# Soft mixture of experts in a vision tower: dispatch of three quarters before the fourth, phi normalised in the prologue, combine logits in two parts

## The chip, the core and the metric

The kernel runs as one program on one core of one Trainium2 chip. The core has TensorE (PE, matmuls, with a weight load PEld for each), VectorE (DVE), ScalarE (ACT), GpSimd (POOL) and SyncE (SP, which here only issues DMAs); each works through its own instruction list in order and waits on semaphores. The metric is the device time of one execution in microseconds (us), as the median of several runs.

## The reference

32 images of 49 tokens with 192 channels go through a tower of two layers: patch embedding, a two-way selective scan (Mamba), a soft mixture of 64 experts, then an RWKV-like attention with its feed-forward, and a transformer block with a mixture of 4 experts. The change is at the soft mixture:

```python
xn = _l2norm(x, axis=2)                      # x is layernorm(h), h after the scan layer
phin = scale * _l2norm(phi, axis=0)          # phi: 192 x 64 experts
logits = jnp.einsum('bmd,dnp->bmnp', xn, phin)
d = jax.nn.softmax(logits, axis=1)           # dispatch: over the 49 tokens of an image
c = jax.nn.softmax(logits.reshape(b_, m_, n_ * p_), axis=-1)   # combine: over the 64 experts
xs = jnp.einsum('bmd,bmnp->bnpd', xn, d)     # the slots: one row per image and expert
h = gelu(einsum('bnpd,ndh->bnph', xs, w1) + b1)
ys = jnp.einsum('bnph,nhd->bnpd', h, w2) + b2
y = jnp.einsum('bnpd,bmnp->bmd', ys, c)
```

## The kernel before

All data is float32. The 1568 tokens are cut into 16 tiles of 98 tokens (two images each); four tiles, eight images, are a quarter, and most work goes by quarters q = 0 to 3.

The selective scan runs in 8 stages of 24 units. Each unit is a multiply and a scan on DVE (L1463, L1474), an exponential on ACT (L1034), a multiply on POOL (L821) and two matmuls on PE that add to a state sum in PSUM; after a channel group's last unit DVE multiplies the sum with its gate (L1524), and PE projects the gated rows out (`out_pe`). After the last unit DVE also took phi to unit length (`unit_phi`, L1489 to L1495: square, sum, a reciprocal root by integer trick and three Newton steps on 64x1 elements, multiply).

Then comes what is called the slot stage here. DVE takes layer-norm statistics and the unit-length factors for tiles 0 to 11 (`FIRST`) and afterwards for tiles 12 to 15 (`LAST`). ACT makes the unit-length rows `xn` (L1146), PE turns them (L1885) and ACT copies the turned rows to `xnT`. From there, for each quarter: PE makes the 64 x 392 dispatch logits; DVE takes the maximum over each image's tokens and subtracts it (L1567, L1568); ACT takes the exp (L1157); DVE sums, inverts and multiplies (L1574 to L1576, the "share"); PE turns the shares back (L2085); DVE spreads them into blocks that keep the two images of a tile apart (L1583, `dbd`, the "masked block"). The slot matmuls follow: 12 groups `s_xs` (three channel strides for each quarter), each copied out of PSUM by ACT or DVE in turn (L923, L1588).

The expert layers take 16 groups of 4 experts. In step g, PE does the second layer of group g-2, the first layer (two halves of the 768 hidden channels) of group g, and the turning of group g-1's hidden rows. The combine logits of all 16 tiles stood in step 0, behind group 0's first layer (`combine_logits`, 96x98 weights, 64 columns); their softmax is on DVE and ACT (L1594, L1595, L1191).

SP issues the weights of the experts in this order, with one fixed wait for each piece of buffer space: the first layers of groups 0, 1 and the second layer of group 0 as soon as the scan stage is out; first layer 2 and second layer 1 once phi is turned; then for each g from 3 the first layer of group g when group g-3's first layer is done (`s_h1`), and the second layer of group g-1 when group g-3's output is done (`s_y2`). The first of these second-layer loads waits for `s_y2` 0, the output of expert group 0.

PSUM has 8 banks; a table (`plan`, `use`) fixes which bank every product uses and which engine takes it out, and PE waits before it fills a bank until the former product has been taken.

The small parameters are loaded in the prologue. ACT's first work, the exp of `a_neg` (L941), waits for all loads of the key "small", and its 30 diagonal matrices (L928) follow, then the copies of the first token tiles, for which DVE's first statistics wait.

## Time and profile before

| | us |
|---|---|
| median of 3 runs | 1515.61 |
| lowest and highest run | 1510.67, 1516.45 |
| the profiled execution | 1509.02 |
| its span in the profile | 1507.3 |

| engine | busy us | share of the span | instructions |
|---|---|---|---|
| PE | 1323.9 | 88% | 6684 |
| PEld | 767.2 | 51% | 6684 |
| DVE | 915.8 | 61% | 1513 |
| ACT | 670.9 | 45% | 1206 |
| POOL | 554.6 | 37% | 399 |

The DMA queues moved 151.96 MB; 32 transfers of 2304 KB each are the expert weights. All positions below are us from the start of the span, in one profiled execution. The shares are means over stages with different limits: DVE is busy all the time in the scan stage and PE and DMA in the expert layers. A bracket at the end of a timeline row gives how long the engine was idle before it and which instruction or transfer ended that. A float32 matmul stands as two records in the trace, and a row that is marked x12 is a run of 12 records with a common line and operation.

### The profile page before, as it was taken

The numbers are of one execution on the slowest core, as the hardware profiler recorded it, in microseconds if no ns is written. First come the engines' busy times: TensorE is split into PE (matmuls) and PEld (weight loads), VectorE is DVE, ScalarE is ACT, GpSimd is POOL, SyncE is SP. The second block draws the span as 40 slices with busy tenths as digits, with TensorE's granted clock in tenths as the row PEclk, the third lists the DMA queues.
The fourth block names the chain that finished last, engine by engine and source line by source line (L and its number), as shares of the span: only waits on it lengthen the run. The fifth ranks groups of instructions, "written<-read, shape, count | busy, mean of one in ns | idle before, by whom it ended". The sixth has DMA issues, their size and how long they took to land.

```text
span 1507.3 us, 18440 instructions
## 1 busy us (share of the span) xinstructions
PE 1323.9 (88%) x6684; PEld 767.2 (51%) x6684; DVE 915.8 (61%) x1513; ACT 670.9 (45%) x1206; POOL 554.6 (37%) x399
## 2 busy tenths in 40 slices
PE   7979989898989867469988859979999999999998
PEld 6634445454545434244433445547856659445444
DVE  3789999999999999972100148855446624221022
ACT  4786767677777744042110117631552241313311
POOL 1478898988989887300000020012034302000000
PEclk9999999999999999769999969999999999999999
DMA  6405051422414040344999940000010001030101
GB/s 205 172 2 172 12 162 37 135 75 98 127 46 171 12 160 0 138 178 189 395 397 396 372 103 0 1 0 1 1 38 1 2 1 31 7 110 13 37 0 33
DMA packets 38773, 151.96 MB, mean 101 GB/s; under 512 B 10364, under 2 KB 14587, under 8 KB 33948
## 3 DMA queue, kind: packets, MB, share of 16 engines
q1 hardware_dynamic: 34588, 149.21, 27.6%
q10 hardware_dynamic: 4096, 1.58, 0.4%
q8 instruction: 54, 0.88, 0.2%
q14 instruction: 35, 0.29, 0.1%
HBM read 147.56 MB, written 1.63 MB: 99 GB/s over the span
## 4 chain that ended last, share of the span: by engine, by line
PE 54%; DVE 20%; issue 10%; ACT 6%; DMA 5%; POOL 4%; SPq 1%; ACTq 0%; DVEq 0%; POOLq 0%
PE ps L1876 52%; DVE arena L1474 7%; DVE arena L1463 5%; DMA arena<-in_e_b 4%; POOL arena L821 3%; ACT arena L923 2%; ACT ps L1034 1%; DVE stats L1371 1%; DVE arena L1759 1%; PE ps L1885 1%; ACT arena L928 1%; DVE arena L1483 1%; SPq L633 1%; DVE arena L1763 0%; DVE arena L1514 0%
## 5 line engine op out<-in xcount | busy, mean ns | idle before, releaser
L1876 PE MATMUL ps<-arena 128*32 128x192 f32 (+17 forms) x5236 | 946.4, 415 | 97.8 <-DVE arena L1524 22.2
L1876 PEld LDWEIGHTS ps<-arena 128*32 128x32 f32 (+15 forms) x5236 | 539.7, 154 | 475.7 <-issue 277.1
L821 POOL TENSOR_TENSOR arena<-arena 128x784 f32<-128x784 f32 x192 | 368.9, 1935 | 94.0 <-DVE arena L1474 93.4
L1876 PE MATMUL ps<-arena,ident 128*128 128x392 f32 x900 | 349.3, 517 | 48.3 <-POOL arena L821 40.0
L1474 DVE TENSOR_TENSOR_SCAN arena<-ps,arena 128x784 f32<-128x784 f32 x192 | 341.0, 1777 | 2.5 <-ACT ps L1034 2.5
L1876 PEld LDWEIGHTS ps<-arena,ident 128*128 128x128 f32 x900 | 169.6, 196 | 196.5 <-POOL arena L821 70.5
L1034 ACT ACTIVATE ps<-arena 128x384 f32<-128x384 f32 x384 | 207.9, 575 | 114.2 <-DVE arena L1474 113.4
L923 ACT ACTIVATE arena<-ps 128x392 f32<-128x392 f32 (+9 forms) x265 | 124.3, 487 | 294.7 <-PE ps L1876 206.2
L923 ACT ACTIVATE arena<-ps,arena 128x392 f32<-128x392 f32 (+2 forms) x191 | 103.4, 602 | 224.5 <-PE ps L1876 139.1
L1463 DVE TENSOR_TENSOR arena<-ps,arena 128x784 f32<-128x784 f32 x192 | 182.8, 953 | 8.0 <-ACT ps L1060 6.8
L1622 DVE COPY arena<-ps 128x384 f32<-128x384 f32 x32 | 16.3, 552 | 150.7 <-PE ps L2124 150.7
L1852 DVE SCALAR_TENSOR_TENSOR arena<-ps,arena 128x392 f32<-128x392 f32 x16 | 10.0, 626 | 127.3 <-PE ps L1876 112.0
L891 POOL TENSOR_TENSOR h<-h,arena 98x384 f32<-98x384 f32 x8 | 8.0, 996 | 152.5 <-DVE arena L1699 152.5
L907 POOL TENSOR_TENSOR arena<-arena 96x294 f32<-96x294 f32 x64 | 41.6, 681 | 56.8 <-PE ps L1876 53.5
L855 POOL MEMSET arena<- 128x128 f32 x1 | 0.2, 205 | 124.8 <-ACT arena L923 124.8
L873 POOL TENSOR_SCALAR arena<-arena 128x4 f32<-128x4 f32 x1 | 0.2, 236 | 122.7 <-DMA arena<-in_first 122.7
L1885 PE MATMUL ps<-ident,arena 98*96 98x98 f32 x160 | 21.9, 283 | 23.5 <-ACT arena L1146 17.3
L1298 ACT ACTIVATE arena<-arena 113x588 f32<-113x588 f32 x16 | 11.1, 694 | 62.5 <-DVE arena L1763 62.5
L1785 DVE TENSOR_TENSOR arena<-arena,ps 98x192 f32<-98x192 f32 x32 | 11.1, 354 | 45.6 <-PE ps L1876 44.0
L914 POOL TENSOR_TENSOR h<-h,arena 98x192 f32<-98x192 f32 x16 | 9.3, 593 | 71.7 <-DVE arena L1785 71.7
L1885 PEld LDWEIGHTS ps<-ident,arena 98*96 98x96 f32 x160 | 17.4, 145 | 30.6 <-ACT arena L1146 18.8
L923 ACT ACT_TABLE_LOAD x10 | 12.8, 1283 | 45.2 <-PE ps L1876 45.1
(201 smaller groups left out, 861.0 us busy)
## 6 DMA issues: line engine op xcount, KB each, us to landing
arena<-in_e_w SPq DMA_DIRECT2D x32, 2304.0 KB
arena<-bc_rows SPq DMA_DIRECT2D x128, 392.0 KB, 4.8
arena<-in_patches SPq DMA_DIRECT2D x4, 1176.0 KB, 7.5
arena<-comb_rows SPq DMA_DIRECT2D x1, 3136.0 KB, 10.7
arena<-in_mlp_w SPq DMA_DIRECT2D x5, 576.0 KB, 4.6
arena<-arena ACTq DMA_DIRECT2D x128, 12.0 KB, 8.6
...
```

The costliest lines, as they stand in the source:

```text
L633: sp.dma_start(dst, src).then_inc(loaded[key], 16)
L821: pool.tensor_tensor(pair(hbuf[:, at % SLOTS, :]), pair(hbuf[:, at % SLOTS, :]), c_all[:, n:n + 2, :], ALU.mult).then_inc(times_c, 1)
L907: pool.tensor_tensor(kblk[:, 4 * (i % 2) + 2 * j + c, :].rearrange("p (h l) -> p h l", l=TOKENS), kT[:, c, at:at + TOKENS].unsqueeze(1).br ...
L923: act.activation(dst, src, func, **kw).then_inc(s.taken["act"], 1)
L928: ins = act.activation(dst[r][:, k, :], ident[:, :], ACT.Copy, scale=values(k))
L1034: ins = act.activation(steps_of(two(DECAY[at % 2], 128, HALF)[:, j * QT:(j + 1) * QT])[:, :, lo:lo + TOKENS - 1], steps_of(dt[:, s % 2, c, ...
L1371: own.step(dve.bn_stats(stats[:, t, :], src[:, i, :]))
L1463: TT(pair(hbuf[:, at % SLOTS, :]), bank(DU_BANK, 128, 0, QT).unsqueeze(1).broadcast_to([128, 2, QT]), b_all[:, 2 * p:2 * p + 2, :], ALU.mu ...
L1474: dve.tensor_tensor_scan(hbuf[:, at % SLOTS, :][:, way], dA[:, way], hbuf[:, at % SLOTS, :][:, way], 0.0, ALU.mult, ALU.add).then_inc(scan ...
L1622: dve.tensor_copy(hidT[:, g % 2, 3 * k:3 * k + 3, :].rearrange("p k n -> p (k n)"), bank(s_hT.banks[i][0], 128, 0, 384)).then_inc(s_hT.tak ...
L1876: return pe.matmul(dst, lhsT, rhs, start=first, stop=last)
L1885: ins = pe.transpose(bank(s.banks[i][0], parts, t * TILE, (t + 1) * TILE), src[:, 4 * q + t, chunk(c)], ident[0:TILE, 0:TILE])
```

## The change

Three things are changed, and the numbers of instructions stay as they are but for those of ACT and DVE that change places.

1. `unit_phi` moves on DVE from behind the last scan unit to the prologue, ahead of the first token statistics. Its two loads (phi and scale) move on SP to the end of the group "small", before the second patch load, and so ACT and DVE wait for 12 loads of that key.
2. Dispatch goes by three quarters and then the fourth. ACT copies the turned rows of quarter 0 out after eight tiles. PE turns the shares of quarters 0 to 2, does nine slot groups, then turns quarter 3's shares and does the last three groups. DVE does the softmax of quarters 0 to 2 first. ACT copies slot tiles 0 to 8 and 10, DVE 9 and 11; the PSUM banks are planned anew.
3. The combine logits are made in two parts: tiles 0 to 7 on PE behind the third quarter's dispatch logits, tiles 8 to 15 where all 16 stood before.

On PE, the slot stage and the beginning of the expert layers, in order; L1876 makes all matmuls, L1885 turns `xn`, L2085 the shares. Before:

```order
L1885 MATMUL ps<-ident,arena 96x98 x24
L1876 MATMUL ps<-arena 64x392 x6
L1885 MATMUL ps<-ident,arena 96x98 x8
L1876 MATMUL ps<-arena 64x392 x2
L2085 MATMUL ps<-ident,arena 98x64 x16
L1876 MATMUL ps<-arena 64x64 x96
L1876 MATMUL ps<-arena 128x384
L1876 MATMUL ps<-arena 32x384 x12
L1876 MATMUL ps<-arena 128x384
L1876 MATMUL ps<-arena 32x384 x12
L1876 MATMUL ps<-arena 98x64 x32
L1876 MATMUL ps<-arena 128x384
```

And now (the lines are L1915, L1924 and L2125 there):

```order
L1924 MATMUL ps<-ident,arena 96x98 x24
L1915 MATMUL ps<-arena 64x392 x6
L1915 MATMUL ps<-arena 98x64 x16
L1924 MATMUL ps<-ident,arena 96x98 x8
L1915 MATMUL ps<-arena 64x392 x2
L2125 MATMUL ps<-ident,arena 98x64 x12
L1915 MATMUL ps<-arena 64x64 x72
L2125 MATMUL ps<-ident,arena 98x64 x4
L1915 MATMUL ps<-arena 64x64 x24
L1915 MATMUL ps<-arena 128x384
L1915 MATMUL ps<-arena 32x384 x12
```

Sixteen of the 32 combine-logit matmuls (98x64) now stand ahead of the turning of the fourth quarter, and four turns of the shares stand between the 72nd and the 73rd slot matmul (64x64).

On ACT, from the unit-length rows to the first slot copies; L923 copies out of PSUM, L1146 makes `xn`, L1157 is the dispatch exp. Before:

```order
L1146 ACTIVATE arena<-h,nmean,rs_tmp 98x192 x12
L923 ACTIVATE arena<-ps 96x392 x6
L1146 ACTIVATE arena<-h,nmean,rs_tmp 98x192 x4
L923 ACTIVATE arena<-ps 96x392 x2
L1157 ACTIVATE arena<-arena 64x392 x4
L1158 ACT_TABLE_LOAD
L1158 ACTIVATE act_c<-act_c 128x1
L923 ACTIVATE arena<-ps 128x8x32 x6
```

And now (L926, L1149, L1162; L1168 is the combine exp):

```order
L1149 ACTIVATE arena<-h,nmean,rs_tmp 98x192 x8
L926 ACTIVATE arena<-ps 96x392 x2
L1149 ACTIVATE arena<-h,nmean,rs_tmp 98x192 x4
L926 ACTIVATE arena<-ps 96x392 x4
L1149 ACTIVATE arena<-h,nmean,rs_tmp 98x192 x4
L1162 ACTIVATE arena<-arena 64x392 x2
L926 ACTIVATE arena<-ps 96x392 x2
L1162 ACTIVATE arena<-arena 64x392
L1168 ACTIVATE arena<-arena 98x512
L1162 ACTIVATE arena<-arena 64x392
L1182 ACT_TABLE_LOAD
```

Two dispatch exps now precede the copies of the fourth quarter's turned rows, the third stands behind them, and the fourth behind the exp of the first combine half.

The diff, with the bank plan cut to two of its lines and the unchanged bodies of the functions left out:

```diff
@@ -413,11 +413,14 @@
...
-        plan(s_dT, 4, (6, 7), "dve")
+        plan(s_dT, 3, (7, 0, 1), "dve")
...
@@ -650,14 +653,14 @@
                 load("small", dt_b[r], a[f"{p}_b_dt"])
                 load("small", d_skip[r], a[f"{p}_d"])
                 load("small", a_neg[r], a[f"{p}_a_log"])
+            load("small", phiT, a["phi"])
+            load("small", scale_b, a["scale"].partition_broadcast(NE))
             patch_load(1)
             mamba_load(0)
             patch_load(2)
             patch_load(3)
             load("gb", g_row, a["ln_g"].partition_broadcast(TILE))
             load("gb", b_row, a["ln_b"].partition_broadcast(TILE))
-            load("gb", phiT, a["phi"])
-            load("gb", scale_b, a["scale"].partition_broadcast(NE))
             mamba_load(1)
             for r, p in enumerate(("fwd", "bwd")):
                 load("wout", w_out[r], a[f"{p}_w_out"])
@@ -936,7 +939,7 @@
 
                 return lambda k: d_skip[r][:, k:k + 1]
 
-            act.wait_ge(loaded["small"], 16 * 10)
+            act.wait_ge(loaded["small"], 16 * 12)
             for r in range(2):
                 act.activation(a_neg[r], a_neg[r], ACT.Exp).then_inc(aneg_exp, 1)
             act.wait_ge(const_ready, 1)
@@ -1145,18 +1148,39 @@
...
-                for i in range(tiles.start // 2, tiles.stop // 2):
-                    q, c = divmod(i, 2)
+
+            def turned_xn(q):
+
+                for c in range(2):
+                    i = 2 * q + c
                     copy_out(s_xnT, i, xnT[:, c, quarter(q)], bank(s_xnT.banks[i][0], CH, 0, QT))
 
-            unit_tiles(FIRST)
-            unit_tiles(LAST)
-            for q in range(NQ):
+            def dispatch_exp(q):
+
                 s_dl.wait_taken(act, q)
...
+
+            def combine_exp(k):
+
+                s_cl.wait_taken(act, k)
+                v = clog[:, 8 * k:8 * k + 8, :]
+                act.activation(v, v, ACT.Exp).then_inc(cexp, 1)
+
+            unit_tiles(range(0, 2 * TQ))
+            turned_xn(0)
+            unit_tiles(range(2 * TQ, 3 * TQ))
+            turned_xn(1)
+            turned_xn(2)
+            unit_tiles(LAST)
+            dispatch_exp(0)
+            dispatch_exp(1)
+            turned_xn(3)
+            dispatch_exp(2)
+            combine_exp(0)
+            dispatch_exp(3)
...
-            for i in range(0, 12, 2):
+            for i in (0, 1, 2, 3, 4, 5, 6, 7, 8, 10):
                 copy_out(s_xs, i, *slots_of(i))
 
             def expert_out(g):
@@ -1185,10 +1209,7 @@
                         copy_out(s_h1, i, hid_e[:, g % 2, k * QH:(k + 1) * QH],
                                  bank(s_h1.banks[i][0], 128, 0, QH), ACT.Gelu)
                 if g == 0:
-                    for k in range(2):
-                        s_cl.wait_taken(act, k)
-                        v = clog[:, 8 * k:8 * k + 8, :]
-                        act.activation(v, v, ACT.Exp).then_inc(cexp, 1)
+                    combine_exp(1)
             expert_out(NG - 1)
 
             act.wait_ge(loaded["rw"], 16 * RW_LOADS)
@@ -1403,6 +1424,19 @@
+            def unit_phi():
+
+                dve.wait_ge(loaded["small"], 16 * 12)
...
+            unit_phi()
@@ -1483,20 +1517,7 @@
-            def unit_phi():
...
             for at in SCHEDULE:
-                if at == LOOPED:
-                    unit_phi()
@@ -1568,32 +1590,49 @@
...
 
-            for q in range(NQ):
+            def dispatch_share(q):
+
...
-            dve.wait_ge(const_ready, MIX_CONST)
+
             both = mask2.unsqueeze(1).broadcast_to([TILE, TQ, 2, NE])
-            for q in range(NQ):
+
+            def dispatch_blocks(q):
+
...
                     .then_inc(s_dT.taken["dve"], 1)
-            for i in range(1, 12, 2):
-                s_xs.wait_filled(dve, i)
-                dve.tensor_copy(*slots_of(i)).then_inc(s_xs.taken["dve"], 1)
-
-            for k in range(2):
+
+            def combine_less(k):
+
...
+
+            dve.wait_ge(const_ready, MIX_CONST)
+            for q in range(3):
+                dispatch_less(q)
+            for q in range(3):
+                dispatch_share(q)
+            combine_less(0)
+            dispatch_less(3)
+            for q in range(3):
+                dispatch_blocks(q)
+            dispatch_share(3)
+            dispatch_blocks(3)
+            for i in (9, 11):
+                s_xs.wait_filled(dve, i)
+                dve.tensor_copy(*slots_of(i)).then_inc(s_xs.taken["dve"], 1)
+            combine_less(1)
 
             def combine_weights():
 
@@ -2053,15 +2092,14 @@
                              c == 0, c == 1)
                 ins.then_inc(s_dl.filled, 1)
 
-            def combine_logits():
-
-                for k in range(2):
-                    s_cl.fill(pe, k)
-                    for t in range(8):
-                        for c in range(2):
-                            ins = mm(bank(s_cl.banks[k][0], TILE, t * NE, (t + 1) * NE),
-                                     xnT[:, c, cols(8 * k + t)], phin[:, c, :], c == 0, c == 1)
-                    ins.then_inc(s_cl.filled, 1)
+            def combine_logits(k):
+
+                s_cl.fill(pe, k)
+                for t in range(8):
+                    for c in range(2):
+                        ins = mm(bank(s_cl.banks[k][0], TILE, t * NE, (t + 1) * NE),
+                                 xnT[:, c, cols(8 * k + t)], phin[:, c, :], c == 0, c == 1)
+                ins.then_inc(s_cl.filled, 1)
 
             def combine_turn(q):
 
@@ -2075,9 +2113,11 @@
             turned_xn(range(6))
             for q in range(3):
                 dispatch_logits(q)
+            combine_logits(0)
             turned_xn(range(6, 8))
             dispatch_logits(3)
-            for q in range(NQ):
+            def dispatch_turn(q):
+
                 pe.wait_ge(dnorm, q + 1)
                 s_dT.fill(pe, q)
                 for t in range(TQ):
@@ -2086,8 +2126,13 @@
                                        dlog[:, 2 * i:2 * i + 2, :].rearrange("p i l -> p (i l)"),
                                        ident[0:NE, 0:NE])
                 ins.then_inc(s_dT.filled, 1)
+
+            for q in range(3):
+                dispatch_turn(q)
             for i in range(12):
                 grp, c = divmod(i, 3)
+                if i == 9:
+                    dispatch_turn(3)
                 s_xs.fill(pe, i)
                 s_dT.wait_taken(pe, grp)
                 for t in range(TQ):
@@ -2146,7 +2191,7 @@
                 if g < NG:
                     expert_hidden(g)
                 if g == 0:
-                    combine_logits()
+                    combine_logits(1)
                 if 1 <= g <= NG:
                     expert_turn(g - 1)
             for k in range(2):
```

## Rows read from the trace of the kernel before

**Rows 1.** Windows by stage: us, busy per engine, PEclk, DMA share, GB/s

```profile
657.00:686.00 29.00, 21.83 (x267) 14.56 (x269) 13.99 (x28) 8.45 (x15) 0.00 (x0) 0.76 0.01 1
...
704.00:861.00 157.00, 138.18 (x1475) 64.12 (x1476) 15.07 (x29) 18.51 (x45) 3.64 (x18) 0.96 1.01 396
```

**Rows 2.** Timeline, SP and PE: start, us, engine, line, operation, count [idle <-releaser]

```profile
702.85 0.33 SPq L633 DMA_DIRECT2D arena<-in_e_w  x1
...
868.18 4.97 PE L1876 MATMUL ps<-arena 4*128 4x192 f32 x50 [2.06 <-DMA arena<-in_e_b]
```

**Rows 3.** Timeline, last scan to the out-projection's sums

```profile
612.59 0.53 DVE L1489 TENSOR_TENSOR arena<-arena 64x192 f32<-64x192 f32 x1
...
614.88 1.59 PE L1876 MATMUL ps<-arena,ident 128*128 128x392 f32 x4 [0.33 <-POOL arena L821]
...
619.59 0.55 DVE L1524 TENSOR_TENSOR arena<-ps,arena 128x392 f32<-128x392 f32 x1
620.07 3.20 DVE L1371 BATCH_NORM_STATS2 stats<-arena 98x6 f32<-98x192 f32 x12
...
620.19 6.74 PE L1876 MATMUL ps<-arena 128*98 128x192 f32 x24 [3.72 <-DVE arena L1524]
...
624.46 0.35 DVE L1483 TENSOR_TENSOR arena<-arena,ps 98x192 f32<-98x192 f32 x1 [0.94 <-PE ps L1876]
```

**Rows 4.** Window of PE alone: us, busy, PEclk, DMA share, GB/s

```profile
618.00:619.00 1.00, 0.00 (x0) 0.84 0.00 0
```

**Rows 5.** Timeline of the slot stage

```profile
657.79 0.97 PE L1885 MATMUL ps<-ident,arena 98*96 98x98 f32 x8
...
658.43 0.88 ACT L923 ACTIVATE arena<-ps 96x392 f32<-96x392 f32 x2 [1.56 <-PE ps L1885]
658.49 0.56 DVE L1568 TENSOR_TENSOR arena<-ps,arena 64x392 f32<-64x392 f32 x1
...
662.02 0.54 DVE L1574 TENSOR_REDUCE arena<-arena 64x8 f32<-64x392 f32 x1
...
667.19 1.27 DVE L1583 TENSOR_TENSOR arena<-ps,arena 98x512 f32<-98x512 f32 x2
...
669.17 9.41 PE L1876 MATMUL ps<-arena 98*64 98x64 f32 x192
...
679.32 19.02 PE L1876 MATMUL ps<-arena 4*128 4x384 f32 x168 [0.74 <-ACT arena L923]
```

**Rows 6.** Groups by form, 668 to 700 us: busy, mean ns, idle before

```profile
L1876 PE MATMUL ps<-arena 96*98 96x64 f32 x64 | 5.8, 251 | 0.0
...
L1583 DVE TENSOR_TENSOR arena<-ps,arena 98x512 f32<-98x512 f32 x3 | 2.0, 681 | 0.2 <-PE ps L2085 0.2
L1594 DVE TENSOR_REDUCE arena<-ps 98x8 f32<-98x512 f32 x2 | 1.4, 692 | 11.9 <-PE ps L1876 11.9
...
L2085 PE MATMUL ps<-ident,arena 64*98 64x64 f32 x8 | 1.2, 310 | 2.6 <-DVE arena L1583 2.6
```

**Rows 7.** Window of PE alone, first hidden layer of the experts

```profile
680.00:684.00 4.00, 4.00 (x26) 0.57 0.00 0
```

**Rows 8.** Timeline of PE, hidden layers of two later groups

```profile
780.75 9.17 PE L1876 MATMUL ps<-arena 4*128 4x384 f32 x52 [1.80 <-DMA arena<-in_e_b]
...
842.60 5.88 PE L1876 MATMUL ps<-arena 4*128 4x384 f32 x52 [0.61 <-DMA arena<-in_e_b]
```

**Rows 9.** Timeline of the prologue

```profile
6.12 0.43 SPq L633 DMA_DIRECT2D arena<-in_bwd_a_log  x1
...
7.58 15.65 PE L1876 MATMUL ps<-arena 128*98 128x192 f32 x84 [7.58 <-DMA arena<-in_patches]
...
9.46 0.38 ACT L941 ACTIVATE arena<-arena 128x48 f32<-128x48 f32 x2 [7.37 <-DMA arena<-in_bwd_a_log]
...
11.31 0.61 SPq L633 DMA_DIRECT2D arena<-in_scale  x1
...
18.92 1.14 DVE L1371 BATCH_NORM_STATS2 stats<-h 98x6 f32<-98x192 f32 x4 [8.57 <-ACT h L923]
```

28 lines of the change are left out of this document (15 added, 13 removed).

## The prediction

> **What bounds the kernel now.** I read the windows by stage first, then the waits and the timeline around the places that the change touches. The change sits between the selective scan (to about 616 us) and the expert layers (from 679 us). In the expert layers the DMA engines are full from 704 to 861 us at 396 GB/s [rows 1]: that stretch lasts as long as 26 weight loads last (26 of the 32 loads of 2304 KB each, 2.36 MB, at 396 GB/s: 155 us), and no engine can shorten it. But before it the DMA is idle: 1 GB/s from 657 to 686 us [rows 1], and after one load again until 702.85. The weights for the first expert groups are long there, and the next loads may only go when buffers come free. The stream starts when SP issues at 702.85, on the signal of the first expert output, s_y2 0 [rows 2], and its last load is what the last expert output waits for at 868.18 [rows 2]. So the rule for this change is: whatever brings the first expert output forward by X brings the end forward by X, and nothing behind it matters, since after 868 us the code is the same and follows in a chain. The first expert output is reached by a serial path over DVE, ACT and PE from the last scan on. Before it, the scan stage is DVE without a gap, so a later start of it is paid in full.
>
> **Unit-length phi out of the way.** After its last scan DVE takes phi to unit length, 17 small operations from 612.59 on; behind them, at 619.59, stands the gate L1524 [rows 3], whose input, the last state sum, PE had ready at 614.88 + 1.59 = 616.47 [rows 3]. PE waits 3.72 us for that gate. Without phi the gate goes at 616.5: -3.05 us. There is more: the clock falls to half within 618 to 619 us, in this very gap [rows 4], and the out-projection of the next 6.7 us pays for it; twelve matmul records of 192 columns, two tiles' worth, take 4.2 us there (620.19 to the sum at 624.46), against 2.24 us in the prologue, where 84 take 15.65 us [rows 3, 9]. DVE waits 0.94 us for the second sum [rows 3]. With a gap of only 0.65 us (the gate, 0.55, and two signals) I take the clock to stay up; then PE is done at 617.15 + 2.24 = 619.4, before DVE's twelve statistics (3.20 us) end at 620.3, and the 0.94 goes too. Together -4.0; I take -3.9, bounds -3.0 (clock down all the same) and -4.0.
>
> The gate and the statistics now run beside GpSimd's additions of beta. The small phi operations ran beside them as well. The Trainium skill (SBUF — State Buffer, the part on the shared port pair) says that VectorE and GpSimd exclude each other only where VectorE has two SBUF inputs or a two-port mode; the gate reads one operand from PSUM and the statistics have one input, so by it nothing is added. Were every pairing to block, the gate would wait for at most one addition, some 0.5 us, and the sum would be that much smaller.
>
> **What phi costs in the prologue.** On DVE nothing: it sits idle 8.57 us before its first statistics at 18.92, because ACT first makes 30 diagonals [rows 9]; even the 7.0 us that phi takes at 612.59 fit. The loads are not free. ACT's first exp waits 7.37 us for the last of ten small loads, issued by SP at 6.12 and used at 9.46, 3.3 us later; from there the path goes through ACT's diagonals and first token copies to DVE [rows 9]. Now it is the last of twelve: phi and scale are issued behind it, 0.6 us each (scale 0.61) [rows 9]. If each load lands 3.3 us after its issue, ACT starts 1.1 to 1.2 us later; if the queue was what held the tenth back and the two ride along, as little as 0. I take +0.8, nearer to the issue, bounds 0 and +1.2. It passes through the whole scan stage. The same two issues delay the second patch load by 1.2 us; PE needs it for its fifth tile, at 7.58 + 4 x 2.24 = 16.5 us, some 10 us after its issue, so I put that at 0. By the Trainium skill (DMA: Bandwidth & Descriptors, "Anatomy of one DMA") a small DMA costs about 2.0 us; scale, issued until 7.8, would then be there at 9.8 and the term would be +0.4.
>
> **Half of the combine logits moved.** Sixteen column tiles' logits stand on PE between the first and the second expert's hidden layer: 64 records, 5.8 us, in front of the first expert output [rows 6]. Half of them go ahead, into the slot stage: -2.9 us here. What they cost there is in the next part. The other half's softmax stays off the path: ACT's exp and its table loads lie beside the second hidden layer as before.
>
> **The slot stage, step by step** (times of the trace before). Up to the third quarter's logits nothing changes: PE ends them at 657.8, DVE their subtraction at 658.49 + 0.56 = 659.05 [rows 5]. Then:
> PE now does the first half of the combine logits, 2.9 us, until 660.7, and only then turns the last quarter (0.97); ACT's copies begin 658.43 - 657.79 = 0.64 later and last 0.88 [rows 5]: until 662.2. ACT holds the exp of quarter 2 behind these copies; taken as long as one such copy with its start, 0.5, it is ready at 662.7. DVE's shares cost (667.19 - 662.02) / 4 = 1.29 each [rows 5]: quarters 0 and 1 until 661.6, then a wait of 1.1 us that was not there before, quarter 2 from 662.7 to 664.0. In line behind it: maximum and subtraction of the combine half, 2 x 0.7 [rows 6], until 665.4; subtraction of quarter 3, about 1.15, until 666.6; the first masked block, 0.7 [rows 6], until 667.3. PE begins the slot matmuls at 667.3, where it did at 669.17 [rows 5]: 1.9 us earlier. PE's twelve groups took 9.41 us, 0.78 each [rows 5]. Nine of them last until 674.4. Now comes the new hole: the fourth quarter's turn stands between group 9 and group 10, and group 10 waits for its masked block on DVE. Eight records of turns took 1.2 us, so four take 0.6, and a block 0.68 [rows 6]; with the signals 1.4 us in which PE does nothing else, until 675.8. Three more groups, 2.35 us, until 678.1, and the last copy, 0.74 (669.17 + 9.41 = 678.58 to 679.32): the expert layers begin at 678.85 instead of 679.32. Of the 1.9 us won, 0.5 remain. With all groups at full clock it would be 1.2. I take -0.6. ACT now copies ten of the twelve slot tiles, each shorter than a group, so it keeps up. Bounds: -1.9, if the hole closed, and +1.5, if the combine half ran at half clock and came into the path of quarter 2 with 1.5 to 2 us more.
>
> **The clock at the first expert layer** is a term of its own. It fell in 680 to 684 us to 0.57 [rows 7], since the PE had been thinly used; a half-clock stretch makes the hidden layers of one group, 5.88 us otherwise, take 9.17 us: 3.3 us [rows 8]. How it falls in the new order can't be read from before: from -1.7 (it stays up) to +3.3 (one such stretch more). I take 0.
>
> **Sum.** -3.9 + 0.8 - 2.9 - 0.6 = -6.6 us. The profiled execution took 1509.02 us (span 1507.3), so it becomes 1502.4. The median of the runs, 1515.61, lies 6.6 us above that execution; I subtract from the median: 1509.0 us.
>
> **Rivals.**
> (a) PE's clock takes part of it back. The hole before group 10 and the short wait after group 12 keep PE at half clock over all of the first hidden layer: +3.3, giving 1512.3. For it: the clock did fall just there [rows 7], and the new hole makes it more likely. Against: the combine half fills a stretch in which PE idled.
> (b) The clock stays up through the first hidden layer, and the slot stage gains its 1.2: -6.6 - 1.7 - 0.6 = -8.9, 1506.7.
> (c) Slower than before, by one mechanism: PE at half clock from the first slot group to the first expert output. Slot groups cost +1.0, the first hidden layer (7.5 us before, 11.8 at half clock all along) +4.3, the remaining combine half +2.9, the second hidden layer +5.9: 14 us against a gain of 6.6, so 1523. It decides from 6.6 us of lost clock on, that is from 13 us of dense work at half clock. Against it: in the DMA-bound stage the clock came back within one group's work [rows 8]. The Trainium skill (TensorE: Matmul & The Clock Gate, "The HAM clock gate") calls the throttled state the default and says that sustained activity releases it; by this rule the dense hidden layers end the half-clock stretch, which speaks against (c) and for (a) as the most that the clock can take.
> (d) The change does not do what it is read to do: an earlier first output doesn't advance the end, as the DMA stream makes it up (its loads slower, or held by another signal). Then only the prologue's +0.8 shows: 1516.4. Against it: 26 loads stand behind one signal, with idle DMA ahead of it [rows 1, 2].
>
> **Numbers.** Chances: forecast 0.58, (a) 0.13, (b) 0.14, (c) 0.05, (d) 0.10. A measurement of this kernel can tell 0.5%, 7.6 us, from no change; the three runs of before alone lie 5.8 us apart. The forecast is at 6.6, just inside that, so "faster by over 0.5%" gets (b) and something under half of the forecast: 0.40. Slower: (c) and a little scatter, 0.07. Within: 0.53. The range reaches from 1501.5 (all lower bounds, -4.0, 0, -2.9, -1.9 and the clock's -1.7, come to -10.5, and the scatter of the runs) to 1516 (a and most of d).
>
> **What the profile after would show.** The DVE gate right behind PE's last state sum, with PE's wait before the out-projection under 1 us and the clock at 1.00 there; phi's 17 operations between 10 and 16 us, and DVE's first statistics about 0.8 us later; PE idle 1.4 us before the tenth slot group, ACT's third exp behind the last turned copies; 2.9 us of combine logits between the hidden layers; SP's first load on s_y2 about 6.6 us earlier, and the last expert output as much earlier. I am wrong if the stream starts earlier and ends no earlier, if the first statistics of DVE move by more than 1.5 us, or if the hole before the tenth group is not there.

## The result, and the profile after

| | before | after |
|---|---|---|
| median of 6 runs, us | 1515.3 | 1508.13 |
| lowest and highest run | 1510.67, 1516.45 | 1504.82, 1509.44 |
| the profiled execution, its span | 1509.02, 1507.3 | 1508.46, 1506.7 |

The ratio is 0.9952, with a 95% interval of 0.9938 to 0.9965: 7.2 us faster by the medians, where 6.6 were forecast (1509.0 us). The two profiled executions differ by 0.6 us only, so the first question is where 6.6 us went between them. The end of a stage is easier to compare than the end of the run. Counted from the end of the last state sum, which itself scatters between 614.2 and 616.5 us among the executions of this study, the places are:

| us from the end of the last state sum | before | after | difference |
|---|---|---|---|
| unit-length rows begin (ACT) | 27.47 | 23.44 | -4.03 |
| first expert layer (PE) | 62.85 | 58.85 | -4.00 |
| load on s_y2 0 (SP) | 86.38 | 77.95 | -8.43 |
| load on s_y2 1 (SP) | 98.43 | 91.65 | -6.78 |
| mix matmuls, behind the last expert output (PE) | 267.22 | 260.45 | -6.77 |

In absolute positions the mix matmuls begin at 876.28 instead of 883.69, 7.41 us earlier, and up to 1268 us the distance stays 7.37 us within 0.05. Most of it is lost around 1290 us, in code that the change doesn't touch.

The places that answer to [rows 3], timeline of DVE and PE after: start, us, engine, line, operation, count, and in brackets the idle time before with what ended it.

```profile
614.24 1.59 PE L1915 MATMUL ps<-arena,ident 128*128 128x392 f32 x4 [0.22 <-POOL arena L824]
...
615.94 0.57 DVE L1545 TENSOR_TENSOR arena<-ps,arena 128x392 f32<-128x392 f32 x1 [3.80 <-PE ps L1915]
...
616.56 2.19 PE L1915 MATMUL ps<-arena 128*98 128x192 f32 x12 [0.73 <-DVE arena L1545]
620.03 2.16 PE L1915 MATMUL ps<-arena 128*98 128x192 f32 x12 [1.28 <-DVE arena L1517]
```

The gate stands 0.1 us behind the sum, PE waits 0.73 us where it waited 3.72, and twelve records of the projection take 2.19 and 2.16 us, full clock. The granted clock is 1.00 from 614 to 620 us. The second twelve wait 1.28 us for a free bank, which DVE's twelve statistics hold up. What was 27.47 us to the unit-length rows is now 23.44.

The slot stage, against [rows 5]:

```profile
658.14 0.56 DVE L1597 TENSOR_REDUCE arena<-arena 64x8 f32<-64x392 f32 x1 [0.88 <-ACT arena L1162]
658.73 0.20 DVE L1598 RECIPROCAL arena<-arena 64x8 f32<-64x8 f32 x1
658.96 0.56 DVE L1599 TENSOR_TENSOR arena<-arena 64x392 f32<-64x392 f32 x1
659.44 0.68 DVE L1617 TENSOR_REDUCE arena<-ps 98x8 f32<-98x512 f32 x1
660.15 0.69 DVE L1618 TENSOR_TENSOR arena<-ps,arena 98x512 f32<-98x512 f32 x1
...
662.64 7.74 PE L1915 MATMUL ps<-arena 98*64 98x64 f32 x144 [2.55 <-DVE arena L1608]
670.31 0.43 PE L2125 MATMUL ps<-ident,arena 64*98 64x64 f32 x4
671.62 2.35 PE L1915 MATMUL ps<-arena 98*64 98x64 f32 x48 [0.88 <-DVE arena L1608]
674.68 14.58 PE L1915 MATMUL ps<-arena 4*128 4x384 f32 x136 [0.72 <-ACT arena L926]
```

DVE waits 0.88 us for the third exp, then takes 1.37 us for the combine part (L1617, L1618) ahead of everything of quarter 3. PE begins the slot groups at 662.64; with the 4.67 us by which the stage began earlier that is 667.31 on before's scale, where 667.3 was forecast. The nine groups take 7.74 us, 0.86 each, since they begin at half clock (granted clock 0.50 from 664 to 668 us), and the hole ahead of the tenth is 671.62 - (662.64 + 7.74) = 1.24 us. So all that was won ahead of the slot groups is spent behind their start.

Windows of all engines that answer to [rows 1], of the first and the third group's hidden layer ([rows 7]), and the load and the last expert output of [rows 2]. Ahead of the last three numbers, PEclk, DMA share and GB/s, stands the busy time of each engine:

```profile
652.00:681.00 29.00, 24.20 (x314) 17.62 (x313) 13.20 (x26) 12.22 (x22) 0.00 (x0) 0.88 0.01 3
695.00:854.00 159.00, 140.09 (x1477) 64.78 (x1478) 15.08 (x30) 18.71 (x45) 3.64 (x18) 0.95 1.00 392
676.00:680.00 4.00, 4.00 (x45) 1.33 (x38) 0.00 (x0) 0.49 (x1) 0.00 (x0) 1.00 0.01 4
696.00:700.00 4.00, 4.00 (x27) 0.99 (x25) 0.00 (x0) 0.47 (x1) 0.00 (x0) 0.58 0.94 395
```

```profile
693.78 0.33 SPq L636 DMA_DIRECT2D arena<-in_e_w  x1
...
861.45 4.97 PE L1915 MATMUL ps<-arena 4*128 4x192 f32 x50 [2.63 <-DMA arena<-in_e_b]
```

The picture of an idle DMA ahead of the load on s_y2 0 and a full one behind it is the same (3 and 392 GB/s). The first group's hidden layer is at full clock now: 5.92 us from its start to SP's load on its end, against 7.58. But the third group's falls to 0.58 and takes 7.53 us instead of 5.88. That is the step from -8.43 to -6.78 in the table. PE waits 1.23 us ahead of it in both kernels, before first:

```profile
704.02 0.56 PE L2071 MATMUL ps<-ident,arena 98*128 98x98 f32 x4 [1.23 <-DVE arena L1612]
704.50 5.88 PE L1876 MATMUL ps<-arena 4*128 4x384 f32 x52
```

```profile
694.95 0.56 PE L2109 MATMUL ps<-ident,arena 98*128 98x98 f32 x4 [1.23 <-DVE arena L1651]
695.44 7.53 PE L1915 MATMUL ps<-arena 4*128 4x384 f32 x52
```

So the wait alone doesn't decide it. PE was busy for 2.65 of the 4 us from 700 in before and for 2.77 of the 4 us from 692 in after, both at clock 1.00. Among the experiments the clock stayed up here in phi_only and before_tail_fill, whose slot stage is the old one, and fell in every kernel with a new order that kept this wait. Why it falls in these and not in the others is not shown.

And the place where the profiled pair comes together again. The four-row gate logits of the last stage, in before and in after, PE's timeline:

```profile
1295.33 14.77 PE L1876 MATMUL ps<-arena 128*4 128x392 f32 x48 [2.33 <-ACT arena L923]
```

```profile
1287.96 19.16 PE L1915 MATMUL ps<-arena 128*4 128x392 f32 x48 [2.33 <-ACT arena L926]
```

Both wait the same 2.33 us for the same ACT copies. In before the clock stayed up (1.00) and 48 records took 14.77 us; in after it fell (0.50 from 1288 to 1296 us) and they took 19.16, and the 16 records behind them 6.08 instead of 4.39: 6.1 us that no instruction of the change explains. Another 0.7 us go between 1325 and 1352 us; nothing here traces them. The executions of before scatter over 6 to 10 us between runs; the one with the profile was a quick one (1509.02 against a median of 1515.3). It is the only profile of that kernel as it stands, so that its usual execution has the late half clock is argued from these times, and not seen.

### The profile page after: what moved, and what is told of

The parts are those of the page before. It is cut to its first block, busy times and chain, and to the rows that moved or that the text cites. A ratio compares the mean times of both kernels' runs of the same rounds, so it can differ in the third digit from the quotient of the medians.

```text
span 1506.7 us, 18440 instructions
## 1 busy us (share of the span) xinstructions
PE 1324.3 (88%) x6684; PEld 763.3 (51%) x6684; DVE 911.4 (60%) x1509; ACT 673.4 (45%) x1210; POOL 553.1 (37%) x399
## 4 chain that ended last, share of the span: by engine, by line
PE 51%; DVE 20%; issue 11%; ACT 6%; POOL 6%; DMA 5%; SPq 1%; ACTq 0%; DVEq 0%; POOLq 0%
PE ps L1915 49%; DVE arena L1508 7%; DVE arena L1497 5%; DMA arena<-in_e_b 4%; POOL arena L824 4%; ACT arena L926 2%; ACT ps L1037 1%; DVE stats L1392 1%; DVE arena L1798 1%; PE ps L1924 1%; SPq L636 1%; ACT arena L931 1%; DVE arena L1517 1%; POOL arena L835 1%; POOL arena L839 1%
## 5 line engine op out<-in xcount | busy, mean ns | idle before, releaser
L1915 PE MATMUL ps<-arena 64*32 64x384 f32 (+17 forms) x5236 | 948.6, 416 | 100.2 <-ACT arena L926 22.4
L1915 PEld LDWEIGHTS ps<-arena 64*32 64x32 f32 (+15 forms) x5236 | 537.3, 154 | 483.0 <-issue 288.6
L1915 PE MATMUL ps<-arena,ident 128*128 128x392 f32 x900 | 348.3, 515 | 50.9 <-POOL arena L824 42.7
L1915 PEld LDWEIGHTS ps<-arena,ident 128*128 128x128 f32 x900 | 169.1, 195 | 199.2 <-POOL arena L824 74.2
L926 ACT ACTIVATE arena<-ps 128x392 f32<-128x392 f32 (+9 forms) x269 | 126.7, 489 | 284.7 <-PE ps L1915 203.4
L926 ACT ACTIVATE arena<-ps,arena 128x392 f32<-128x392 f32 (+2 forms) x191 | 103.4, 602 | 229.6 <-PE ps L1915 144.8
L1924 PE MATMUL ps<-ident,arena 98*96 98x98 f32 x160 | 22.5, 283 | 23.3 <-ACT arena L1149 17.6
L1924 PEld LDWEIGHTS ps<-ident,arena 98*96 98x96 f32 x160 | 17.4, 144 | 30.4 <-ACT arena L1149 19.6
```

The costliest lines, as they stand in the source:

```text
L926: act.activation(dst, src, func, **kw).then_inc(s.taken["act"], 1)
L1915: return pe.matmul(dst, lhsT, rhs, start=first, stop=last)
L1924: ins = pe.transpose(bank(s.banks[i][0], parts, t * TILE, (t + 1) * TILE), src[:, 4 * q + t, chunk(c)], ident[0:TILE, 0:TILE])
```

## Experiments

All are compared with the kernel before, run on the same chip beside them. "From the last sum" is the measure of the table above. Most experiments were profiled once, so a position tells of one execution; how much it means can be seen from kernels that are the same up to there. after, after_again and tail_fill have the first expert layer at 58.85, 58.86 and 58.83 and the load on s_y2 0 at 77.95, 77.96 and 77.93, but the mix matmuls at 260.45, 260.23 and 259.05; before and before_tail_fill have 62.85 and 86.38 both, and the mix matmuls at 267.22 and 265.69. So the mix column scatters by 1.5 us.

| kernel | median us (runs) | ratio, 95% interval | first expert layer | s_y2 0 | mix | mix to store |
|---|---|---|---|---|---|---|
| before | 1514.1 to 1515.3 | 1 | 62.85 | 86.38 | 267.22 | 440.8 |
| after | 1508.13 (6) | 0.9952, 0.9938 to 0.9965 | 58.85 | 77.95 | 260.45 | 446.9 |
| phi_only | 1511.17 (12) | 0.9984, 0.9964 to 1.0004 | 59.21 | 82.74 | 263.61 | 447.2 |
| split_only | 1517.45 (12) | 1.0036, 1.0020 to 1.0052 | 67.63 | 88.42 | 269.59 | 447.8 |
| unsplit | 1506.58 (7) | 0.9946, 0.9926 to 0.9967 | 56.36 | 78.23 | 259.28 | 448.0 |
| after_again | 1507.50 (8) | 0.9955, 0.9938 to 0.9972 | 58.86 | 77.96 | 260.23 | 441.1 |
| swap | 1505.99 (6) | 0.9941, 0.9924 to 0.9959 | 58.85 | 77.95 | 259.70 | 447.6 |
| tail_fill | 1503.60 (6) | 0.9924, 0.9907 to 0.9941 | 58.83 | 77.93 | 259.05 | 445.3 |
| before_tail_fill | 1507.83 (6) | 0.9954, 0.9937 to 0.9971 | 62.85 | 86.38 | 265.69 | 444.7 |
| late_split | 1504.13 (6) | 0.9925, 0.9907 to 0.9944 | | | | |
| late_split_2 | 1504.75 (6) | 0.9941, 0.9927 to 0.9954 | 55.45 | 74.54 | 256.54 | 447.4 |
| swap_fill | 1500.94 (5) | 0.9919, 0.9906 to 0.9933 | 58.82 | 77.92 | 257.44 | 442.8 |
| order_only | 1501.29 (5) | 0.9914, 0.9900 to 0.9927 | 54.48 | 73.64 | 252.64 | 447.8 |
| best | 1494.84 (4) | 0.9877, 0.9863 to 0.9891 | 54.46 | 73.63 | 252.56 | 441.7 |

"Mix to store" is the time from the mix matmuls to SP's store of the combine rows of the last stage; 441 means the clock stayed up over the gate logits.

The scatter of the mix column goes with the clock over the last expert output ahead of it. At half clock (granted clock 0.50) its 50 records take 4.97 us; that was so in before, after, after_again, phi_only and order_only. In the other profiles they took 2.65 us, in tail_fill as here:

```profile
860.48 2.65 PE L1915 MATMUL ps<-arena 4*128 4x192 f32 x50 [2.11 <-DMA arena<-in_e_b]
```

So like is best compared with like: the first five with after and before, the others with tail_fill and before_tail_fill. The change itself is worth 6.77 us in the one pair and 6.64 in the other.

### The parts alone

**phi_only.** The kernel before with the prologue's and SP's part of the diff and nothing else.

```diff
+            load("small", phiT, a["phi"])
+            load("small", scale_b, a["scale"].partition_broadcast(NE))
             patch_load(1)
...
+            unit_phi()
             def tokens_normed(k):
...
-                if at == LOOPED:
-                    unit_phi()
```

> The kernel before with only phi moved to the prologue (its two loads at the end of the group small, its operations on DVE ahead of the first token statistics). Theory A (every us that the end of the scan stage gains is carried through the expert stage to the end): gate 3.7 us earlier (near 615.9 instead of 619.59), the second-layer load on s_y2 0 as much earlier or a little more (its first projection group ran at half clock before: 698 to 699), median 3.5 to 4.5 us below before. Rival B (the expert weights' stream sets its own end, so that an earlier start is lost by 850 us): gate as early, the last expert output at the same time as before, median within 1 us of before. Rival C (a move changes which stretches the clock is lowered in, and that decides): median anywhere between 3 us above and 10 us below, without the load on s_y2 0 and the end moving together.

The gate stands at 615.8, PE's projection at 616.47 behind a wait of 0.73 us. The first expert layer comes 3.64 us, the s_y2 0 load 3.64 us, the mix matmuls 3.61 us earlier (from the last sum): the stage passes the gain on unchanged (the last expert output is at half clock in both), and theory B falls. The clock at the first hidden layer fell here as in before (0.57). By the median it is 3.0 us below before, under the 3.5 to 4.5 expected, with an interval that includes no change (0.9964 to 1.0004); the positions carry the verdict for theory A, not the median. In this profile the late gate logits ran at half clock, so its span is 2.7 us longer than that of before.

**split_only.** The kernel before with the combine logits in two parts, and the dispatch in its old order.

```diff
             for q in range(3):
                 dispatch_logits(q)
+            combine_logits(0)
             turned_xn(range(6, 8))
             dispatch_logits(3)
...
-                    combine_logits()
+                    combine_logits(1)
```

> The kernel before with only the combine logits in two parts: the first eight tiles behind the third dispatch logits, the last eight in step 0; the dispatch runs as before, in the order of four quarters. Theory A: step 0 is 2.9 us shorter by its matmuls, and the first hidden layer that followed at half clock (680 to 684, 0.57) may be at full clock; s_y2 0 falls 2.5 to 4.5 us earlier (698.4 to 700.4), median 2.5 to 4.5 us below before. Rival B: the load on s_y2 0 earlier, last expert output not, median within 1 us of before. Rival D (the 2.9 us return in the slot stage since the combine matmuls and their exp stand ahead of the last quarter's work): first expert layer begins 2 to 3 us later than 679.32 and the median is that of before.

Rival D, and more than it said: the first expert layer comes 4.78 us later. Timeline of DVE and PE in split_only:

```profile
662.05 0.56 DVE L1573 TENSOR_REDUCE arena<-ps 64x8 f32<-64x392 f32 x1 [4.65 <-PE ps L1887]
...
669.84 1.23 PE L2096 MATMUL ps<-ident,arena 64*98 64x64 f32 x8 [4.86 <-DVE arena L1591]
```

In the old order DVE takes no share before the subtraction of quarter 3 is done. The combine matmuls hold up quarter 3's turning, DVE waits 4.65 us, and then PE waits 4.86 us for DVE's combine subtraction, whose bank (by the kernel's bank table) the second turned share needs. Theory A for this part is wrong: by itself it makes the kernel slower, 1.0036 with the whole interval above 1. The mix matmuls stand 3.9 us behind those of before_tail_fill.

**unsplit.** The changed kernel with all combine logits in step 0 again, so phi and the order of the quarters alone.

```diff
-            combine_logits(0)
             turned_xn(range(6, 8))
...
                 if g == 0:
+                    combine_logits(0)
                     combine_logits(1)
```

> The changed kernel with the combine logits undivided in step 0 again: phi in the prologue and dispatch of three quarters ahead of the fourth stay. Theory A: the slot stage's reordering is worth nothing to 1 us, so the median lies 3.5 to 5 us below before and 3 to 4.5 us above the changed kernel; the first expert layer begins 0 to 1 us earlier than the 674.68 of the changed kernel, since DVE has no combine part between the quarters and ACT no third exp more. Rival E (the reordering is worth 1.9 us that the early combine part eats up in the changed kernel): first expert layer near 672.8, median 6 us below before and only 1 us above the changed kernel.

Neither as a whole: the first expert layer is at 672.40, as rival E had it, but the median is 7.6 us below before and 0.9 us below that of the changed kernel, not above.

```profile
660.56 7.53 PE L1914 MATMUL ps<-arena 98*64 98x64 f32 x144 [1.33 <-DVE arena L1607]
668.02 0.43 PE L2123 MATMUL ps<-ident,arena 64*98 64x64 f32 x4
669.33 2.35 PE L1914 MATMUL ps<-arena 98*64 98x64 f32 x48 [0.88 <-DVE arena L1607]
672.40 17.36 PE L1914 MATMUL ps<-arena 4*128 4x384 f32 x168 [0.72 <-ACT arena L925]
```

From the last sum, the slot groups begin 2.3 us earlier than in the changed kernel. The reordering by three quarters brings the first expert layer 2.85 us nearer (59.21 to 56.36); the split takes 2.49 of it (58.85) and gives 2.77 back in step 0 (s_y2 0 at 78.23 and 77.95). So at the load on s_y2 0 the split is worth 0.3 us, and the reordering, with the first hidden layer that it brings to full clock, 4.5 (82.74 to 78.23). At the mix matmuls the kernel without the split stands at 259.28, beside 259.05 of tail_fill, with the last expert output at full clock in both: the split is worth 0.2 us there, which is nothing.

**after_again.** The changed kernel, unchanged, on this chip.

> The changed kernel once more, on the chip of the other three. If theory A holds: 6 to 8 us below before by the medians, whatever the profiled pair shows. The profiled execution of before had the four-column matmuls of the late gate (near 1296 us) at full clock and that of the changed kernel had them at half clock, 6 us longer at the same instructions. Rival C (this lowering comes with the changed kernel's shifted times and is the price of the change): the stretch is at half clock again here and at full clock in the execution of before. Theory A': it falls in most executions of both kernels, and the profiled one of before was one of the few without it (its 1509.02 stands 6.3 us below the median of before).

```profile
1288.07 14.77 PE L1915 MATMUL ps<-arena 128*4 128x392 f32 x48 [2.33 <-ACT arena L926]
```

The same kernel, the same wait of 2.33 us, and this time 14.77 us. Its span is 1500.0 us, 6.7 below that of its first profile; up to 1268 us the two agree within 0.3 us. So the changed kernel doesn't always pay the late half clock (rival C falls), and a profiled pair can differ by the whole size of the effect.

### The late half clock

**tail_fill and before_tail_fill.** Three matmuls whose result nothing reads, in PE's wait ahead of the gate logits.

```diff
                 packed(s_xmT, xb_, lambda i: pe.wait_ge(xm_ready, i + 1), range(4 * hf, 4 * hf + 4))
+                if hf == 1:
+                    s_lT.fill(pe, 0)
+                    for _ in range(3):
+                        mm(bank(s_lT.banks[0][0], 128, 0, QT), ident[:, :], xmA[:, quarter(0)], True, True)
```

> The changed kernel with three matmuls (identity by 392 columns, 0.66 us each, their result not read) in PE's 2.33 us wait ahead of the four-row gate logits near 1286 us. Theory A' (this wait is followed by half clock in most executions and not in all: four of six profiled executions of these kernels had it, each with 6.1 to 7 us more between the mix matmuls and the store of the combine rows): that stretch is at full clock in the profile, mix matmuls to store 441 us (446.9 in the changed kernel's first profile, 441.1 in its second), the median 4 to 6 us below the changed kernel, near 1502. Rival V (the lowering has another cause than this wait): store of the combine rows 446 to 448 us behind the mix matmuls again, median that of the changed kernel.

> The kernel before with the same three matmuls in the same wait. Theory A': its median falls as far, by 4 to 6 us to 1508 to 1511, so that the distance of 7 us between the two kernels is the same with the filling in both. Rival C (the late lowering belongs to the changed kernel and the medians' distance hides it): the median falls by under 2 us here while it falls by 4 to 6 us in the changed kernel.

```profile
1288.04 2.17 PE L1915 MATMUL ps<-arena,ident 128*128 128x392 f32 x6
1290.52 14.77 PE L1915 MATMUL ps<-arena 128*4 128x392 f32 x48 [0.32 <-ACT arena L926]
```

The wait shrinks to 0.32 us, and the gate logits run at full clock in both kernels: 14.77 us here. The changed kernel falls to 1503.60 us, 3.9 below after_again (which ran on another occasion; 4.7 by the two ratios), and before to 1507.83, 7.4 below its own median. Theory A' holds in direction for both, though neither profile has the 441 us that it wanted between the mix matmuls and the store. The filling adds work and the kernel gets faster. What stays unclear: with the filling in both, the two kernels lie 4.2 us apart and not 7. They ran side by side and their times don't overlap (1500.3 to 1505.2, 1506.87 to 1509.99), so a distance there is; six runs of each are too few to tell 4 from 7. The mix-to-store time is 445 and not 441 in these two profiles, since the clock fell elsewhere in that stretch: in tail_fill it stood at 0.50 and 0.58 from 996 to 1004 us, in before_tail_fill at 0.67 and 0.50 from 1308 to 1316.

### Where the slot stage loses its gain

**late_split.** The first combine part goes into PE's waits for the shares; DVE's half stands behind the fourth block, ACT's exp in step 0.

```diff
-            combine_logits(0)
             turned_xn(range(6, 8))
...
-            for q in range(3):
+            dispatch_turn(0)
+            combine_logits(0)
+            for q in range(1, 3):
                 dispatch_turn(q)
...
-            combine_less(0)
             dispatch_less(3)
...
             dispatch_blocks(3)
+            combine_less(0)
```

> The changed kernel with the first part of the combine logits moved: PE makes it behind the first turned share instead of behind the third dispatch logits, DVE takes its maximum and subtracts behind the fourth masked block, ACT takes its exp in step 0. Theory F (in the changed kernel this part costs 2.3 us of the slot stage: 1.37 us of DVE ahead of the fourth quarter's maximum, and 0.88 us since the third exp stands behind the turned copies; the kernel with undivided combine logits began its first expert layer at 672.40 against 674.68): first expert layer at 672.3 to 673.0, load on s_y2 0 at 691.2 to 692.0 instead of 693.78, first load of the late weights (w_kvr) 1.5 to 2.5 us earlier than 853.41. Rival G (the matmuls of the part cost their 2.9 us wherever they stand): first expert layer at 674.5 or later, load on s_y2 0 at 693.8. By the median either lies within 3 us of the changed kernel; the positions decide.

The profiled execution of this run was at a clock of 0.547 from end to end and took 2267 us; the other five took 1500.72 to 1505.93 us, and the ratio is that of these five. It was run once more for its positions.

> The kernel of late_split once more, since the only profiled execution of it had the clock lowered from its first to its last us and shows no positions. The same numbers: theory F: first expert layer at 672.3 to 673.0 and load on s_y2 0 at 691.2 to 692.0; rival G: 674.5 or later, and 693.8. The median again about 3 us below the changed kernel if F holds and the rest of the expert stage passes the gain on; within 1 us of it if the expert stage swallows it, as it did with the 5 us of swap.

```profile
655.81 2.98 PE L1916 MATMUL ps<-arena 96*98 96x64 f32 x32
658.73 0.65 PE L2125 MATMUL ps<-ident,arena 64*98 64x64 f32 x8
659.34 6.61 PE L1916 MATMUL ps<-arena 98*64 98x64 f32 x144
665.88 0.43 PE L2125 MATMUL ps<-ident,arena 64*98 64x64 f32 x4
667.18 2.35 PE L1916 MATMUL ps<-arena 98*64 98x64 f32 x48 [0.87 <-DVE arena L1609]
```

The combine part (32 records, 2.98 us) stands where PE waited. Theory F, and more: the first expert layer comes 3.40 us nearer, since PE without its 2.55 us wait also does the nine slot groups in 6.61 us instead of 7.74. The mix matmuls are 3.91 us nearer than in after; but the last expert output ran at full clock here, and against tail_fill, where it did too, 2.51 us of the 3.40 remain.

**order_only.** Beside late_split, the fourth share's turn ahead of the seventh group and the first half of the combine weights in step 0.

```diff
-                if i == 9:
+                if i == 6:
                     dispatch_turn(3)
...
             combine_less(1)
+            combine_weights(0)
...
-                    combine_weights()
+                    combine_weights(1)
```

> Of the kernel best only its three changes of order on PE, DVE and ACT: the combine logits' first part behind the first turned share, the fourth share turned ahead of the seventh slot group, the first half of the combine weights in step 0. No filling matmuls and the order of the expert weights as in the changed kernel. Theory H (the hole ahead of the tenth slot group is worth what the prediction gave it, 1.2 to 1.4 us, and the 1.23 us of PE ahead of the first combine turn are what lets the clock fall over the third group's hidden layer): from the last state sum to the first expert layer 54.4 us as in best (55.45 with late_split alone, 58.85 in the changed kernel), no wait over 0.3 us between the ninth and the tenth group, the third group's hidden layer 5.88 us instead of 7.53, and the mix matmuls 253 to 255.5 us behind the last state sum against 256.5 with late_split alone and 260.4 in the changed kernel. Median 1500 to 1504. Rival X (the stream of weights takes the earlier start back, as with swap): mix matmuls 256 us or more behind the last state sum, median as late_split, near 1504.

```profile
660.68 4.49 PE L1916 MATMUL ps<-arena 98*64 98x64 f32 x96
665.09 0.43 PE L2125 MATMUL ps<-ident,arena 64*98 64x64 f32 x4
665.45 4.43 PE L1916 MATMUL ps<-arena 98*64 98x64 f32 x96
...
689.65 0.56 PE L2110 MATMUL ps<-ident,arena 98*128 98x98 f32 x4
690.14 5.88 PE L1916 MATMUL ps<-arena 4*128 4x384 f32 x52
```

Theory H. The hole is gone, and with it 0.97 us. The 1.23 us of waiting ahead of the first combine turn (in after at 694.95) is gone too, and the third group's hidden layer is at full clock: 5.88 us. That this wait was the cause fits, but in before the same wait of 1.23 us was followed by full clock. The mix matmuls come 7.8 us nearer than in the changed kernel, a little more than expected, and the median is 1501.29 us, 13 below before.

### The stream of expert weights

**swap.** First layers of group g ahead of second layers of group g-2.

```diff
-            for g in range(3, NG + 1):
+            for g in range(3, NG + 2):
                 if g < NG:
                     s_h1.wait_filled(sp, 2 * (g - 3) + 1)
                     first_layers(g)
-                s_y2.wait_filled(sp, g - 3)
-                second_layers(g - 1)
+                if g > 3:
+                    s_y2.wait_filled(sp, g - 4)
+                    second_layers(g - 2)
```

> The changed kernel with one change in SP's order of the expert weights: from group 4 on the first layers of group g stand ahead of the second layers of group g-2 (before: behind them), so that each load is behind its own wait alone. The DMA engines stood nearly idle from 688 to 693.8 (15 to 78 GB/s). Theory S (the end of the expert stage follows the start of the unbroken stream of expert weights): the first layers of group 4 are issued near 689.3 instead of 694.5, the w_kvr load 4 to 5.5 us earlier than 853.41 (848 to 849.5), the median 4 to 5.5 us below the changed kernel. Rival T (PE's own 10.4 us for each group is what the stage takes): w_kvr within 1 us of 853.4, median that of the changed kernel. Rival U (the swapped order lets PE wait for second layers that come one place later): a wait of PE for in_e_w or in_e_b of 3 us or more between 710 and 760, and a gain under 2 us.

Theory S misses: the load is issued at 689.12, as expected, PE waits for no weights before 760 us, and still w_kvr is issued at 853.60, and the mix matmuls stand at 259.70, 0.5 to 0.8 us nearer than in after and after_again and 0.65 farther than in tail_fill. That is no gain that can be told from scatter. Rival T's two numbers hold (w_kvr within 1 us, the ratio 0.9941 beside 0.9955), but its reason does not: PE is not busy all the time, it waits for weights. Of rival U the small gain came and the early waits did not. Later PE does wait for weights, and pays behind the waits. A row of x102 is one group's output and the next one's hidden layer, 8.46 us at full clock:

```profile
780.68 10.10 PE L1916 MATMUL ps<-arena 4*128 4x192 f32 x102 [2.55 <-DMA arena<-in_e_b]
...
805.53 10.09 PE L1916 MATMUL ps<-arena 4*128 4x192 f32 x102 [3.47 <-DMA arena<-in_e_b]
...
830.25 13.01 PE L1916 MATMUL ps<-arena 4*128 4x192 f32 x102 [3.21 <-DMA arena<-in_e_b]
```

**swap_fill.** Two matmuls more per group, from the tenth on, ahead of the wait for weights.

```diff
                 b = g % 3
+                if g >= 9:
+                    s_h1.fill(pe, 2 * g)
+                    for _ in range(2):
+                        mm(bank(s_h1.banks[2 * g][0], 128, 0, QH), ident[:, :], xsT[:, 0, 0:12, :].rearrange("p n i -> p (n i)"), True, True)
                 pe.wait_ge(loaded[f"w1e{b}"], 16 * 2 * (g // 3 + 1))
```

> The kernel swap with, in each expert group from the tenth on, two matmuls (identity by 384 columns, 1.3 us together, their result not read) ahead of PE's wait for that group's weights. In swap three of these waits (2.55, 3.47, 3.21 us) were followed by half clock, with 1.6, 1.6 and 4.5 us more for the hidden layer behind them, and the DMA engines fell to 0.93 after 800 us. Theory W (the 4.7 us that swap's stream was ahead were lost to half clock behind PE's waits for weights): those hidden layers take 5.8 us each, DMA share 1.0 until the end, w_kvr at 849 to 850.5 and mix matmuls near 871 to 872.5, median 2 to 4 us below swap. Rival T (PE's own work is the bound): the fillings come on top, w_kvr at 855 or later, median slower than swap by 2 us or more. Rival X (the stream of weights is at its rate of some 395 GB/s and no more is to be had than swap got): w_kvr within 1 us of 853.6, no half clock, median as swap.

Windows of swap and of swap_fill: PEclk, DMA share and GB/s are the last three numbers.

```profile
800.00:850.00 50.00, 41.55 (x418) 19.46 (x414) 4.09 (x8) 4.92 (x12) 0.00 (x0) 0.86 0.93 366
```

```profile
800.00:850.00 50.00, 45.40 (x466) 21.30 (x462) 4.09 (x8) 5.24 (x12) 0.00 (x0) 1.00 0.99 391
```

Theory W in the main: all hidden layers from the tenth group on take 5.88 us, the clock is 1.00 and the DMA is back at 0.99. The mix matmuls come 2.26 us nearer than in swap, 3.01 nearer than in after and 1.61 nearer than in tail_fill; the last expert output ends 4.9 us nearer than in after (from the last sum, 245.65 against 250.59), of which 2.3 are that output's own half clock in after, but the wait behind it, for the stored outputs, is 11.79 us instead of 9.86. The w_kvr load missed its forecast: at 852.11, not 849 to 850.5; the mix matmuls, at 872.74, just missed theirs. The median is 5.1 us below that of swap (3.3 us by the two ratios), more than the positions give up to the mix matmuls; in this profile the gate logits ran at full clock, which makes another 4.8.

**best.** All of it.

> The changed kernel with all of these: the combine logits' first part behind the first turned share (late_split), the order of expert weights of swap, the fillings of swap_fill and tail_fill, the fourth share turned ahead of the seventh slot group instead of the tenth, and the first half of the combine weights taken in step 0. If the gains add: 2 us from the slot stage, 1.4 us from the earlier turn (PE has no wait ahead of the tenth group), 0 to 4 us from the expert stage, 4 us from the late gate: median near 1498, 17 us below before, between 1494 and 1502. If each frees a wait that another takes up again: as tail_fill, near 1503. The 1.23 us of waiting ahead of the first combine turn is gone if the weights' first half is what it waited for.

1494.84 us, 0.9877 of before (0.9863 to 0.9891), inside the range for gains that add. But its mix matmuls stand at 252.56 from the last sum, where order_only has them at 252.64: swap and its fillings added nothing to the new order, although the last expert output is at full clock in best and at half in order_only. The 6.4 us between the medians of the two are about those of the late gate logits (mix to store 441.7 against 447.8 us).

## Why the prediction was right

| step | forecast | measured in the profiled pair |
|---|---|---|
| phi out of the way | -3.9 | -4.03: -2.99 to the projection, -1.04 to the unit-length rows |
| phi in the prologue | +0.8 | +0.26 at DVE's first statistics |
| slot stage | -0.6 | +0.03 |
| clock at the first hidden layer | 0 | -1.66 there, +1.65 at the third group's |
| combine half out of step 0 | -2.9 | -2.78 |
| sum | -6.6 | -6.5: -6.77 at the mix matmuls, from the last sum, and +0.26 |

Positions from the last sum leave the prologue's step out; what it did to the scan's end is hidden in a scatter of 1 to 2 us. Without it -7.4 were forecast and -6.77 measured. So the total was closer than its terms, by luck: the prologue was put 0.5 us too dear and the slot stage 0.6 us too cheap, and these two cancel.

**phi** went as worked out, the clock included. Only PE's end was misread: it was to be done at 619.4 and was done at 622.2 (622.8 in the times of before), since its second twelve records wait for a bank; that cost nothing, because the unit-length rows wait for DVE. phi_only has both parts too (0.73 us of wait, projection at full clock), but from the last sum to the first expert layer it gained 3.64, not 4.03: 0.4 us were taken back in the slot stage.

**The prologue** was sized from the wrong row. I took the way from issue to use (3.3 us) as fixed and added two issues. In after, SP's issues and ACT's first exp, against [rows 9]:

```profile
6.66 0.56 SPq L636 DMA_DIRECT2D arena<-in_phi  x1
7.26 0.59 SPq L636 DMA_DIRECT2D arena<-in_scale  x1
...
9.72 0.38 ACT L944 ACTIVATE arena<-arena 128x48 f32<-128x48 f32 x2 [7.63 <-DMA arena<-in_scale]
```

Scale is issued at 7.26 and ACT starts at 9.72: 2.46 us, against 9.46 - 6.12 = 3.34 us for the tenth load before. So two loads cost 0.26 us. The tenth had waited behind larger ones: the token weights and the first patches fill the DMA engines from 3 to 7 us (a share of 0.92 to 1.16 in each us of before). The ten small loads are issued about 0.47 us apart, and from issue to landing they take 5.8 us for the first and ever less, down to 3.3 for the tenth, so they land about 0.2 us apart. In after the tenth takes 2.9 us, phi 2.7 and scale 2.4, with a DMA share of 0.21 from 8 to 9 us. That is the case of the lower bound, in which the two ride along. The Trainium skill (DMA: Bandwidth & Descriptors, "Anatomy of one DMA") gives about 2.0 us of fixed cost for a DMA, on the path issued by GpSimd, and these loads are issued by SP; scale's 2.4 us are the nearest to it here, and the term by it, +0.4, was nearer than mine.

**The slot stage** was right to the tenth of a us where it was read from rows (slot groups at 667.3), and the hole was there (1.24 us for 1.4). It came out 0.6 short because nine groups at 0.86 us replaced nine at 0.78: behind the wait of 2.55 us the clock was down. late_split_2, without that wait, did them at full clock in 6.61 us.

**The clock term**, taken as 0 between -1.7 and +3.3, is the step that was right by cancellation. The half clock went out of the first hidden layer (-1.66), where I had looked for it, and into the third group's (+1.65), behind a wait of 1.23 us, where I had not. Rival (b) had the first of these, but not its gain in the slot stage; rival (a) expected the opposite at the first hidden layer, and no rival had the third group's.

**The end follows the first expert output**: right for the change, -6.77 at the mix matmuls for -6.78 at the load on s_y2 1, and for phi_only, so rival (d) falls. But -8.43 at the first expert output itself, s_y2 0, became -6.77, so "whatever brings the first expert output forward by X" holds only as far as the clock behind it stays the same; in late_split_2 3.4 us became 2.5 with the last output at full clock in both. But the reason that I gave, that the stream of loads alone sets the end, doesn't hold: swap began it 5 us earlier and won nothing to speak of. Half clock behind PE's waits for weights is one cause, since filling them gave 2.3 us back; the rest stays open.

**The medians.** I subtracted from the median, and that was the right base: the profiled execution of before was one of those without the late half clock. The prediction gave no reason for the choice, so this was luck. Had I forecast the profiled pair, 1502.4 against 1508.46, the reasons would have been right and the number wrong.
